# Decay attention: a pair's two heads issue their score products in turns, behind one common wait

## The reference, cut to what matters

```python
qkv = silu(x @ qkv_w.T)                       # q, k, v per head, width 64
aw = einsum('bhid,bhjd->bhij', qi, ki) * dd   # scores, times a decay by distance
intra = einsum('bhij,bhjd->bhid', aw, vi)     # times the values
...
attn = rmsnorm(all heads, norm_w)
out = (sigmoid(x @ gate_w.T) * attn) @ out_w.T
```

## Time and profile before

| | us |
|---|---|
| median of three runs | 1342.32 |
| lowest and highest | 1339.06, 1342.86 |
| span of the profiled execution | 1339.6 |
| decay attention, 16 turns, within it | 314.4 to 702.9 |
| one turn | 24.3 |
| mean granted TensorE clock over the span | 0.974 of 2.4 GHz |

### The profile page before, as it was taken

The page is one execution under the profiler, slowest core; times in us unless marked ns, Lnnn a source line. Parts: engine busy times, 40 slices in busy tenths (PEclk is TensorE's granted clock), DMA queues, the critical chain, the costliest instruction groups (busy, mean ns, idle before and its releaser), DMA issues. The chain is left out here.

```text
span 1339.6 us, 23090 instructions
## 1 busy us (share of the span) xinstructions
PE 1227.5 (92%) x7690; PEld 986.5 (74%) x7690; DVE 757.1 (57%) x1599; ACT 501.9 (37%) x1124; POOL 398.7 (30%) x379
## 2 busy tenths in 40 slices
PE   9999889889999999999998898998987989899895
PEld 6776556656888888888885687777864788788785
DVE  2545577666334333343346787787866555555545
ACT  4423244444544534435442434433442313232231
POOL 3000400001333333243331444444535043333321
PEclk9999999999999999999998999999989999899897
DMA  3000000002101101101101000000011111110200
GB/s 140 1 1 0 20 1 2 0 0 99 63 32 43 51 31 43 51 31 63 31 31 36 16 21 16 20 16 20 16 47 48 48 48 47 47 47 8 85 0 32
DMA packets 11236, 45.26 MB, mean 34 GB/s; under 512 B 1729, under 2 KB 2753, under 8 KB 9921
## 3 DMA queue, kind: packets, MB, share of 16 engines
q1 hardware_dynamic: 11200, 44.81, 9.7%
HBM read 43.76 MB, written 1.05 MB: 33 GB/s over the span
## 5 line engine op out<-in xcount | busy, mean ns | idle before, releaser
L986 DVE TENSOR_TENSOR d_s_m<-ps,d_decay 128x384 f32<-128x384 f32 x128 | 71.2, 556 | 118.4 <-PE ps L1076 116.1
L1572 DVE TENSOR_TENSOR f_hidl<-f_hid,f_hidh 128x512 fp32r<-128x512 f32 x64 | 95.4, 1490 | 45.0 <-ACT f_hidh L1593 45.0
L111 PE MATMUL ps<-xTl,f_wh 128*128 128x512 f32 x256 | 101.9, 398 | 13.0 <-DVE f_hid L1570 11.2
L1459 POOL TENSOR_TENSOR f_wh<-f_stage,f_nought 128x3072 fp32r<-128x3072 f32 (+1 forms) x11 | 48.2, 4382 | 196.6 <-PE ps L111 182.9
L111 PE MATMUL ps<-xTh,f_wh 128*128 128x512 f32 x256 | 101.3, 396 | 0.0
L111 PE MATMUL ps<-xTh,f_wl 128*128 128x512 f32 x256 | 101.1, 395 | 0.0
L1340 ACT ACTIVATE e_probs<-ps,e_neg_max 128x128 f32<-128x128 f32 (+1 forms) x128 | 52.6, 416 | 112.7 <-DVE e_neg_max L1287 112.7
L120 PE MATMUL ps<-warm 128*128 128x512 bf16 x298 | 79.5, 425 | 13.1 <-PEq L895 4.5
L111 PE MATMUL ps<-f_wl,f_hidh 128*128 128x256 f32 x256 | 76.6, 299 | 15.8 <-DVE y L1562 15.8
L1593 ACT ACTIVATE f_hidh<-f_hid 128x512 fp32r<-128x512 f32 x64 | 40.4, 632 | 124.7 <-DVE f_hid L1570 124.7
L111 PE MATMUL ps<-xTl,d_wh 128*128 128x512 f32 x192 | 77.6, 404 | 0.7
(11 more groups left out here) (314 smaller groups left out, 3435.0 us busy)
## 6 DMA issues: line engine op xcount, KB each, us to landing
f_stage<-in_w_experts SPq DMA_DIRECT2D x8, 1536.0 KB, 6.3
d_stage<-in_w_decay SPq DMA_DIRECT2D x17, 640.5 KB, 3.8
d_decay<-in_decay SPq DMA_DIRECT2D x16, 384.0 KB, 3.0
e_stage<-in_w_grouped SPq DMA_DIRECT2D x5, 640.0 KB, 3.8
e_wo<-in_wo_grouped SPq DMA_DIRECT2D x5, 512.0 KB, 3.5
f_stage<-in_w_experts SPq DMA_DIRECT2D x3, 512.0 KB, 4.8
xT<-in_xT SPq DMA_DIRECT2D x2, 512.0 KB, 5.9
x<-in_x SPq DMA_DIRECT2D x1, 1024.0 KB, 8.8
```

The costliest lines, as they stand in the source:

```text
L111: mm = pe.matmul(out, w(k), x(k), start=(n == 0), stop=(n == 3 * len(ks) - 1))
L986: dve.tensor_tensor(s_m[:, s % 4, :], ps[:, 4 + s % 2, 0:CAUSAL], decay[:, s % 2, :], ALU.mult).then_inc(sm_ready, 1)
L1459: pool.tensor_tensor(self.wh[slot][:, cols], self.stage[:, cols], nought, ALU.add).then_inc(self.w_hi, 1)
L1572: dve.tensor_tensor(hidl[:, s % 2, f, :], hid[:, n % 2, :], hidh[:, s % 2, f, :].bitcast(F32), ALU.subtract).then_inc(lo_ready, 1)
```

## The change

The unit of `scores` becomes the pair of products of one sequence. The two heads' matmuls are issued in turns, first that of head 0, then that of head 1, and the pair waits once: pair 0 for `evac` 8 and the low parts, each later pair b for `sm_ready` 2b, which is both multiplications of the pair before it.

```diff
-                def scores(s):
-                    b, r = s // 2, s % 2 * HD1
-                    if s == 0:
-                        pe.wait_ge(evac, LEAD + 8 * i + 7)
-                    elif s == 1:
+                def scores(b):
+                    if b == 0:
                         pe.wait_ge(evac, LEAD + 8 * i + 8)
+                        pe.wait_ge(qk_lo, LEAD + 4 * i + 4)
                     else:
-                        pe.wait_ge(sm_ready, LEAD + 8 * i + s - 1)
-                    bank = ps[:, 4 + s % 2, :]
-                    rows = slice(r, r + HD1)
-                    if s == 0:
-                        pe.wait_ge(qk_lo, LEAD + 4 * i + 4)
+                        pe.wait_ge(sm_ready, LEAD + 8 * i + 2 * b)
                     queries = slice(b * SEQ, (b + 1) * SEQ)
+                    heads = [(ps[:, 4 + h, :], slice(h * HD1, (h + 1) * HD1)) for h in range(2)]
                     for n, (k, q) in enumerate(((k_hi, q_lo), (k_lo, q_hi), (k_hi, q_hi))):
-                        pe.matmul(bank[:, 0:SEQ], k[rows, b, :], q[rows, queries], start=(n == 0), stop=(n == 2))
-                    pe.matmul(bank[:, SEQ:CAUSAL], k_T[rows, b * SEQ + P:(b + 1) * SEQ], q_T[rows, b * SEQ + P:(b + 1) * SEQ],
-                              start=True, stop=True).then_inc(s_ps, 1)
+                        for bank, rows in heads:
+                            pe.matmul(bank[:, 0:SEQ], k[rows, b, :], q[rows, queries], start=(n == 0), stop=(n == 2))
+                    for bank, rows in heads:
+                        pe.matmul(bank[:, SEQ:CAUSAL], k_T[rows, b * SEQ + P:(b + 1) * SEQ], q_T[rows, b * SEQ + P:(b + 1) * SEQ],
+                                  start=True, stop=True).then_inc(s_ps, 1)
...
                 for step in range(BATCH + 2):
                     if step < BATCH:
-                        scores(2 * step)
-                        scores(2 * step + 1)
+                        scores(step)
```

## The result

The changed kernel takes 1367.9 us in the median (1365.4 to 1369.1, four runs), the kernel before 1341.8 in the same comparison: a ratio of 1.020, with a 95% interval of 1.019 to 1.022. Slower was forecast, 10 us of it; it is 26 us, outside the range. The profiled execution took 1365.4 us at a mean granted clock of 0.970; the three others took longer, at 0.964 to 0.966, so the trace shows somewhat less of the loss than the median.

The account below looks back on a forecast made before the run. The prediction took TensorE to bound a turn of decay attention. A delay of 1.09 us less 2 x 0.22 made 0.65 a turn, 10.4 us in 16 turns: 1352.7 us from a median of 1342.3, range 1346 to 1360.

Parts of the forecast that it names:

- The start of pair 0: Head of a turn: pair 0 waits for the last v and begins at 570.04, with 0.07 us for the wait.
- From pair to pair: Pairs 0 to 2: each next pair waits for both multiplications, a chain of 2.05 us; pair 2 begins 1.09 us later.
- What the turns give back: Pairs 2 and 3: heads issued in turns take 0.79 us to values, not 1.01, saving 0.22 us each.
- covered by 0.20: Pair 3: multiplication 5 is done 2.30 us after pair 2 starts, ahead of pair 3 at 2.50.
- A: Rival, score products: heads issued in turns do not overlap; 2.65 us a turn, up to 42 us, 1385; chance 0.05.
- B: Rival, pairs 2 and 3: heads hardly overlapped before, so turns give more; -7.2 us, 1335; chance 0.03.
- C: Rival, clock in the experts: another number of half-clock stretches, 3.4 us each; two fewer, 1346, chance 0.05.
- D: Rival, attention stage: new TensorE gaps lower the clock, one 6.8 us stretch every turn; 54 us, 1407; chance 0.04.
- The sum: Whole stage: 1.09 - 2 x 0.22 = 0.65 us later in each of 16 turns, 10.4 us.

Follow-up runs that it names:

- changed_with_small_sums: The changed kernel with GpSimd adding 1 column of the squares, not 256, in each of its 64 sums: 1360.2 us, ratio 1.016.
- changed_with_low_part_first: The changed kernel with low parts 0 and 1 placed on DVE ahead of multiplications 4 and 6, not behind them: 1364.0 us, ratio 1.017.
- changed_with_warm_fill: The changed kernel with matmuls of zeros in TensorE's gaps, 2 ahead of pair 0 and 4 between pairs 0 and 1: 1360.5 us, ratio 1.015.
- warm_fill_and_low_part_first: The changed kernel with zero matmuls in the two gaps and low parts 0 and 1 ahead of multiplications 4 and 6: 1351.3 us, ratio 1.009.
- common_wait_in_series: The changed kernel with its common waits, but each pair's heads issued one after the other again: 1379.3 us, ratio 1.030.

## Why the prediction was wrong

**The start of pair 0**: 0.12 behind the last v, as given. Right.

**From pair to pair**: 2.04 and 2.05 against 2.05. Pair 2 began 4.21 us behind the last v, against the 4.22 that the prediction implies. Right.

**What the turns give back** is the first of two steps that failed. The size on TensorE was right: both heads start together, and a pair takes 0.77 to its values. The step then said that pair 3 is "covered by 0.20" and values 3 "again", because it carried the times of multiplications 5 and 7 over from the old trace, low part included. There the low part ran ahead of GpSimd's sum; with values 0 delayed less than pair 2, it runs behind the sum's start and takes 0.81 (counted from the last v, values 0 begin 0.60 later than before, the sum 0.64, pair 2 1.08 and low part 0 1.07). Multiplications 5 and 7 come 0.38 and 0.40 later behind their pairs, the cover of 0.20 is gone, and DVE sets pair 3. Against the forecast, 0.18 is lost there and 0.36 between pair 3 and project 3. With the forecast's 0.65 and 0.02 for the loop's end that makes 1.21, the difference of the two turns shown (1.25 in the median of undisturbed turns). In short, pair 2 begins 1.08 later and the turn ends 1.21 later: the term that was to give back 0.44 a turn cost 0.13 instead. It was off by 0.57 a turn, some 9 us in 16 turns. The sentence "if that cover were gone, each would cost at most the 0.22 it gives" was wrong as well: behind values 3, the delay went through gate 2, low part 2 and gate 3 and took 0.14 more than the 0.22. changed_with_small_sums and changed_with_low_part_first show the cause from both sides, at 24.9 us a turn each.

**Rivals.** A is out: the heads overlap fully. B is out too: pairs in turns save 0.22 to 0.24, no more. C did not matter: outside the stage the profiled execution went from 951.1 to 950.2 us. D, given 0.04 and priced at one fall in every turn, happened in part: four falls in the profiled run, 4.9 us, and changed_with_warm_fill gives back 5.5 to 7.5 us in the median. This is the second step that failed: the sum had no term for the clock, because the rival was treated as all or nothing and left out of the range.

**The sum**: 10.4 from the chain (11.4 measured once the rest is removed), about 9 from the low parts (16 x 0.57, from 25.47 to 24.90; 9.2 us between the medians of changed_with_warm_fill and warm_fill_and_low_part_first), and 5.5 to 7.5 from the clock. Together that is 25 to 28, for the 26 measured (28 from the 1339.9 of the later comparison).

## What to carry to other kernels

A wait that joins two streams should be asked for its chain: while two heads go round in turns, each engine works on one while the other engine has the other, and one wait for both makes the round trip the sum of the links. Here the same issue order gains 0.3% where both banks are free anyway, and loses 2% where they are not, the falls of the clock included. When a delay differs between two engines, look at which of their instructions change places, and whether they share something; a duration read from the old trace holds only in the old company. Gaps on TensorE can cost time even where another engine is the bound: here gaps of 0.4 to 1.2 us in each turn came with falls of the clock, and filling two of them took the falls away.

## What the runs showed of the hardware

- DVE's subtraction of two SBUF tiles (128 x 256) takes 0.42 us alone, 0.81 when it starts 0.20 after a GpSimd addition of 0.73, and 0.62 when it starts 0.39 after it. In both cases it ended 0.28 after the addition. When the two started within 0.01 of each other, GpSimd took 1.01 and DVE 0.41. DVE's multiplication from PSUM with one SBUF tile was not held (0.55 with an addition beside it and without). The Trainium skill, "GPSIMD Engine Reference", section Specifications, says that GpSimd's SBUF interfaces are shared with VectorE, with contention for DVE instructions that have two SBUF inputs. The traces agree, and add the prices: 0.39 us where 0.53 of the addition was left, 0.20 where 0.34 was left.
- Two products of 64 rows in different row halves run fully side by side: from the start of the last product to the values it is 0.78 us for one alone and 0.77 for two in turns. Issued one after the other, the second product's first matmul started ahead of the first product's third (573.28 against 573.39).
- In the changed kernel TensorE was idle for 0.76, 1.20 and 0.40 us before pairs 0, 1 and 2 of an undisturbed turn, and the clock fell to 1.2 GHz in four of the sixteen turns, each time at the end of the gap of 1.2, in stretches of 3.4 or 6.8 us. It did not fall in the stage with 2 and 4 matmuls in the first two gaps, nor with product 0 early. common_wait_in_series, with less idle time in a turn (2.0 us against 2.67), lost more to the clock: six turns were hit, and a long stretch cost 2.8 us where it cost 1.9 in the changed kernel. Which turns are hit, and why more of them there, the runs leave open.
